# Three edits to an MLP pipeline: rounding on ScalarE, moments by the aggregation instruction, and incoming items spread over the light slots

## The reference, cut to what matters

```python
h = layernorm(x1)                       # x1 = x + mamba(...); plain, no weights
for blk in range(3):
    y = h @ W[2*blk].T + bias           # W: 4-bit weights times scales, plus a low-rank product
    y = gelu(layernorm(y) * gamma + beta)
    y = y @ W[2*blk+1].T + bias
    h = y + h
out = x1 + h
```

## Time and profile before

| | |
|---|---|
| device time, 3 runs | 1979.9 us median (1978.9 to 1980.2) |
| span of the profiled execution | 1980.0 us, the page's own figure |
| share of the span busy: PE, DVE, ACT, POOL | 92%, 78%, 64%, 60% |
| MLP items in the span | from about 1527 us on |
| TensorE clock granted there | below 1.0 until 1570 us, 1.0 after that |

### The profile page before, as it was taken

The page is one execution under the profiler, slowest core; times in us unless marked ns, Lnnn a source line. Parts: engine busy times, 40 slices in busy tenths (PEclk is TensorE's granted clock), DMA queues, the critical chain, the costliest instruction groups (busy, mean ns, idle before and its releaser), DMA issues. The chain is left out here.

```text
span 1980.0 us, 36525 instructions
## 1 busy us (share of the span) xinstructions
PE 1819.1 (92%) x12544; PEld 1380.2 (70%) x12544; DVE 1534.9 (78%) x3311; ACT 1260.0 (64%) x2221; POOL 1189.5 (60%) x1032
## 2 busy tenths in 40 slices
PE   5899999999999999999999999999974798988898
PEld 4577776777777777677777776777753677777776
DVE  4777888878778877777777777777635799999986
ACT  3677767776777666777677767777720455555554
POOL 2566666667666655555555555555540687868785
PEclk8899999999999989999999999999985899999999
DMA  4011111111111101111111111110005202012001
GB/s 141 22 39 38 39 48 58 37 42 37 37 37 37 48 28 49 59 39 44 37 37 37 37 48 58 37 42 26 28 11 148 86 1 95 34 41 89 33 12 43
DMA packets 87271, 91.96 MB, mean 46 GB/s; under 512 B 4928, under 2 KB 82448, under 8 KB 87184
## 3 DMA queue, kind: packets, MB, share of 16 engines
q1 hardware_dynamic: 79360, 79.46, 12.4%
q10 hardware_dynamic: 7824, 11.37, 2.3%
HBM read 57.26 MB, written 25.17 MB: 42 GB/s over the span
## 5 line engine op out<-in xcount | busy, mean ns | idle before, releaser
L860 POOL TENSOR_TENSOR L_xc<-L_xpad,L_vec 128x512 f32<-128x512 f32 x160 | 166.2, 1039 | 420.6 <-ACT L_xpad L659 401.3
L381 PE MATMUL L_front<-L_uhi,L_whi 128*128 128x512 f32 x576 | 247.2, 429 | 10.7 <-DVE L_xc L1078 7.3
L530 PE MATMUL L_mix<-L_wo,L_yg 128*128 128x256 f32 x1024 | 238.8, 387 | 3.2 <-POOL L_yg L852 3.2
L381 PE MATMUL L_front<-L_uhi,L_wlo 128*128 128x512 f32 x576 | 229.7, 399 | 0.0
L381 PE MATMUL L_front<-L_ulo,L_whi 128*128 128x512 f32 x576 | 229.7, 399 | 0.0
L1090 DVE TENSOR_TENSOR L_m<-L_dbank,L_gm 128x512 f32<-128x512 f32 x256 | 175.4, 685 | 69.6 <-ACT L_dbank L699 69.1
L530 PEld LDWEIGHTS L_mix<-L_wo,L_yg 128*128 128x128 f32 x1024 | 192.1, 193 | 35.0 <-issue 7.2
L852 POOL TENSOR_TENSOR L_yg<-L_yg,L_sz 128x512 f32<-128x512 f32 x128 | 164.3, 1284 | 85.9 <-DVE L_yg L1105 85.9
L659 ACT ACTIVATE L_xpad<-L_front,L_pbias 128x512 f32<-128x512 f32 x160 | 108.8, 681 | 131.8 <-PE L_front L381 130.9
L697 ACT ACTIVATE L_dbank<-L_dbank 128x512 f32<-128x512 f32 x256 | 148.8, 581 | 46.7 <-PE L_dbank L437 46.6
L1619 POOL TENSOR_TENSOR M_alo<-M_hT,M_ahi 128x512 fp32r<-128x512 f32 x96 | 125.6, 1312 | 75.1 <-DVE M_ahi L1681 75.1
(11 more groups left out here) (174 smaller groups left out, 4912.5 us busy)
## 6 DMA issues: line engine op xcount, KB each, us to landing
h<-L_hres SPq DMA_DIRECT2D x32, 512.0 KB, 3.0
L_hin<-in_x SPq DMA_DIRECT2D x16, 512.0 KB, 4.6
L_hres<-in_x SPq DMA_DIRECT2D x16, 512.0 KB, 3.8
L_cc<-L_xc ACTq DMA_DIRECT2D x64, 128.0 KB, 2.3
L_hin<-h SPq DMA_DIRECT2D x16, 512.0 KB, 4.7
L_hres<-h SPq DMA_DIRECT2D x16, 512.0 KB, 3.8
M_hin<-h SPq DMA_DIRECT2D x16, 512.0 KB, 6.4
M_xin<-in_x SPq DMA_DIRECT2D x16, 512.0 KB, 6.7
```

The costliest lines, as they stand in the source:

```text
L381: last = nc.tensor.matmul(to[:, :], ww[:, kd, tile * P:(tile + 1) * P], a[:, kd, :], start=i == 0, stop=i == len(passes) - 1)
L530: last = nc.tensor.matmul(mix[1 - s][:, (b % 2) * DM:(b % 2 + 1) * DM], yg[:, t, b * P:(b + 1) * P], wo[layer][:, t, :], start=t == 0, sto ...
L860: nc.gpsimd.tensor_tensor(xc[p][:, q, :].rearrange("p (b i) -> p b i", b=NB), xpad[:, q, :, 0:P], vector(layer, "conv_w", q * TAPS, 1).uns ...
```

## The change

1. round_h goes from DVE (tensor_copy) to ACT (activation Copy). In ACT's step n it stands for slot n, behind the copy_in of the same half. It now also waits for the second product of slot n-4 as a whole.
2. combine (seven instructions) is replaced by four bn_aggr, which reduce the six numbers of a bn_stats to mean and variance, then one tensor_scalar that adds EPS; for a block, another tensor_scalar that negates the mean.
3. add_x, in_stats, in_moments, norm_in (DVE) and scale_in (POOL) of a new item no longer stand in the steps of four neighbouring slots. A helper, entering, gives each stage of four items four steps two apart. For rounds after the first: add_x in steps 3, 5, 7, 9; in_stats, in_moments and scale_in in steps 4, 6, 8, 10; norm_in in steps 5, 7, 9, 11. The loads move to slot n+11 and stand behind the store of the same step. PE's order is not changed.
4. In DVE's step, both add_h now stand together ahead of norm_in and add_x, and the in_stats stand between the block_stats.

```diff
+        def entering(n, first, later):
+            turns = UNITS * BLOCKS
+            if 0 <= n + first < UNITS:
+                return n + first
+            round_, at = divmod(n - later, turns)
+            t = UNITS * (round_ + 1) + at // 2
+            return t if n >= later and at % 2 == 0 and at < 2 * UNITS and t < ITEMS else None
...
 @block.sync, step(n):
-                if n >= UNITS:
-                    load_item(n + 8)
                 store(n - 4)
+                load_item(n + 11)
...
 @block.scalar:
+            def round_h(n, kd):
...
+                if block_of(n) == 0:
+                    act.wait_ge(in_copied, 2 * item_of(n) + kd + 1)
+                else:
+                    act.wait_ge(second_done, 2 * (n - UNITS) + 2)
+                    act.wait_ge(h_added, 2 * (n - UNITS) + kd + 1)
+                nc.scalar.activation(ahi[u][:, kd, :], hT[u][:, kd, :], ACT.Copy).then_inc(h_hi, 1)
...
                 copy_in(n, 0)
+                round_h(n, 0)
                 normalise(n - 2, 3)
                 copy_in(n, 1)
+                round_h(n, 1)
                 gelu(n - 2, 0)
...
 @block.gpsimd, block_scale and step(n):
-                nc.gpsimd.tensor_tensor(shift[u][:, :, 0], mom[u][:, 5, :], rstd[u][:, :, 0], ALU.mult).then_inc(b_shift, 1)
+                nc.gpsimd.tensor_tensor(shift[u][:, :, 0], mean[u][:, :], rstd[u][:, :, 0], ALU.mult).then_inc(b_shift, 1)
-                scale_in(n + 2)
+                scale_in(entering(n, 2, 4))
...
 @block.vector, block_moments (in_moments alike, without the mean):
-                combine(nc, dve, stats[u], mom[u], var[u][:, :, 0], b_stats, b_mom, b_var, n, sign=-1)
+                dve.wait_ge(b_stats, NB * n + NB)
+                for b in range(NB):
+                    nc.vector.bn_aggr(mv[u][:, b, :], stats[u][:, b, :]).then_inc(b_mom, 1)
+                dve.wait_ge(b_mom, NB * n + NB)
+                nc.vector.tensor_scalar(var[u][:, :, 0], mv[u][:, :, 1], EPS, None, ALU.add).then_inc(b_var, 1)
+                nc.vector.tensor_scalar(mean[u][:, :], mv[u][:, :, 0], -1.0, None, ALU.mult).then_inc(b_mean, 1)
...
 @block.vector, step(n):
                 block_moments(n - 1)
                 add_h(n - 3, 0)
-                norm_in(n + 1)
-                in_stats(n + 2, 0)
                 add_h(n - 3, 1)
-                add_x(n + 7)
-                in_stats(n + 2, 1)
+                norm_in(entering(n, 1, 5))
+                add_x(entering(n, 7, 3))
+                in_stats(entering(n, 2, 4), 0)
+                in_stats(entering(n, 2, 4), 1)
                 add_out(n - 3, 0)
                 add_out(n - 3, 1)
-                in_stats(n + 2, 2)
-                in_stats(n + 2, 3)
                 block_stats(n, 0)
-                in_moments(n + 2)
+                in_stats(entering(n, 2, 4), 2)
                 block_stats(n, 1)
-                round_h(n + 1, 0)
+                in_stats(entering(n, 2, 4), 3)
                 block_stats(n, 2)
+                in_moments(entering(n, 2, 4))
                 block_stats(n, 3)
-                round_h(n + 1, 1)
```

More of the change, by code:

```diff
@@ L1412, in mlp_items @@
         stats0, var0, rstd0 = (sb(n, [P, NB, c]) for n, c in (("stats0_", 6), ("var0_", 1), ("rstd0_", 1)))
-        mom, mom0 = sb("mom", [P, 6, NB]), sb("mom0_", [P, 6, NB])
+        mv, mv0, mean = sb("mv", [P, NB, 2]), sb("mv0_", [P, NB, 2]), sb("mean", [P, NB])
         lin = [[ctx.enter_context(nc.psum_tensor(f"M_lin{u}{i}", [P, 512], F32)) for i in range(2)] for u in range(UNITS)]
@@ L1421, in mlp_items @@
         b_stats, b_mom, b_var, b_rstd, b_shift = (sem(n) for n in ("b_stats", "b_mom", "b_var", "b_rstd", "b_shift"))
-        b_normed = sem("b_normed")
+        b_mean, b_normed = sem("b_mean"), sem("b_normed")
         b_turned, b_gelu, g_hi, g_lo = (sem(n) for n in ("b_turned", "b_gelu", "g_hi", "g_lo"))
@@ L1436, in held, with held_by @@
             return hin[u][n // (UNITS * BLOCKS) % 2]
+        def held_by(t):
+            return hin[t % UNITS][t // UNITS % 2]
         def runs(n, m=None):
             return 0 <= n < SLOTS and m in (None, block_of(n))
+        def entering(n, first, later):
[5 more added lines that the diff above has]
+            return t if n >= later and at % 2 == 0 and at < 2 * UNITS and t < ITEMS else None
         block = ctx.enter_context(nc.Block())
@@ L1445, in load_item @@
             def load_item(n):
-                if not runs(n, 0):
+                if n < UNITS or not runs(n, 0):
                     return
@@ L1554, in copy_in @@
                 nc.scalar.activation(hT[u][:, kd, :], lin[u][kd][:, :], ACT.Copy).then_inc(in_copied, 1)
+            def round_h(n, kd):
+                if not runs(n):
+                    return
+                u = n % UNITS
+                if block_of(n) == 0:
[4 more added lines that the diff above has]
+                nc.scalar.activation(ahi[u][:, kd, :], hT[u][:, kd, :], ACT.Copy).then_inc(h_hi, 1)
             def normalise(n, b):
@@ L1596, in _, with scale_in @@
         def _(pool):
-            def scale_in(n):
-                if not runs(n, 0):
+            def scale_in(t):
+                if t is None:
                     return
-                t, u = item_of(n), n % UNITS
+                u = t % UNITS
                 pool.wait_ge(n0_var, t + 1)
@@ L1610, in block_scale @@
                 pool.wait_ge(b_rstd, n + 1)
-                pool.wait_ge(b_mom, 6 * n + 6)
-                nc.gpsimd.tensor_tensor(shift[u][:, :, 0], mom[u][:, 5, :], rstd[u][:, :, 0], ALU.mult).then_inc(b_shift, 1)
+                pool.wait_ge(b_mean, n + 1)
+                nc.gpsimd.tensor_tensor(shift[u][:, :, 0], mean[u][:, :], rstd[u][:, :, 0], ALU.mult).then_inc(b_shift, 1)
             def rest_h(n, kd):
@@ L1640, in _, with add_x @@
         def _(dve):
-            def add_x(n):
-                if not runs(n, 0):
+            def add_x(t):
+                if t is None:
                     return
[L1644 to L1649, removed]
+                u = t % UNITS
+                dve.wait_ge(h_in[u], 32 * (t // UNITS + 1))
+                nc.vector.tensor_tensor(held_by(t)[:, :, :], held_by(t)[:, :, :], xin[u][:, :, :], ALU.add).then_inc(x1_done, 1)
@@ L1650, in in_stats @@
+            def in_stats(t, b):
+                if t is None:
                     return
-                t, u = item_of(n), n % UNITS
+                u = t % UNITS
                 if b == 0:
                     dve.wait_ge(x1_done, t + 1)
-                nc.vector.bn_stats(stats0[u][:, b, :], held(n, u)[:, b, :]).then_inc(n0_stats, 1)
-            def in_moments(n):
-                if not runs(n, 0):
+                nc.vector.bn_stats(stats0[u][:, b, :], held_by(t)[:, b, :]).then_inc(n0_stats, 1)
@@ L1658, in in_moments @@
+            def in_moments(t):
+                if t is None:
                     return
[L1659 to L1663, removed]
+                u = t % UNITS
+                dve.wait_ge(n0_stats, NB * t + NB)
+                for b in range(NB):
+                    nc.vector.bn_aggr(mv0[u][:, b, :], stats0[u][:, b, :]).then_inc(n0_mom, 1)
+                dve.wait_ge(n0_mom, NB * t + NB)
+                nc.vector.tensor_scalar(var0[u][:, :, 0], mv0[u][:, :, 1], EPS, None, ALU.add).then_inc(n0_var, 1)
@@ L1664, in norm_in @@
+            def norm_in(t):
+                if t is None:
                     return
-                t, u = item_of(n), n % UNITS
+                u = t % UNITS
                 dve.wait_ge(n0_rstd, t + 1)
-                dve.wait_ge(n0_mom, 6 * t + 6)
+                dve.wait_ge(n0_mom, NB * t + NB)
                 for b in range(NB):
-                    last = nc.vector.tensor_scalar(normed[u][:, b, :], held(n, u)[:, b, :], mom0[u][:, 5, b:b + 1], rstd0[u][:, b, :],
+                    last = nc.vector.tensor_scalar(normed[u][:, b, :], held_by(t)[:, b, :], mv0[u][:, b, 0:1], rstd0[u][:, b, :],
@@ L1670, in norm_in @@
                                                    ALU.subtract, ALU.mult)
                 last.then_inc(n0_done, 1)
[L1673 to L1681, removed]
```

## The result

The changed kernel takes 1966.8 us (median of 4 runs, 1965.0 to 1968.3) against 1980.05 of the kernel before: a ratio of 0.9932, 95% interval 0.9918 to 0.9946. That is 13 us faster, where 27 were forecast.

The account below looks back on a forecast made before the run. DVE was taken to set the heavy slots, with PE's floor at 7.02 us a slot. Three rounds saving 5.5+2.55 each (24.2) plus 2.6 in the last light set gave 26.8 off 1980.0: 1953 us, range 1938 to 1970.

Parts of the forecast that it names:

- (a): Rival: near PE's floor, scale_in and add_x find gaps, light slots 7.2 us, heavy 9.3; 1940 us; chance 0.12.
- (b): Rival: heavy slots gain, light ones stay at 8.02 us; 1962 us; chance 0.22 shared with another rival.
- (c): Rival: norm_in held behind POOL's subtractions, odd light slots 12.2 us; 2007 us; chance 0.08, of which 0.06 a loss.
- part 4: Light slots with incoming work: add_x and norm_in in odd ones, scale_in in even; 7.7 us each, 2.55 saved a round.
- the rule weighed there: Small float32 DVE operations may share ports with POOL; by it norm_in would wait up to four times behind subtractions.
- DVE sets them: Heavy slots before the change: DVE busy 10.3 to 10.6 us against PE's 9.1, so DVE bounds them.
- Part 1: round_h to ACT: DVE loses 1.8 us a slot; the light slot's own loop falls from 7.58 to 7.15 us.
- Part 2: Moments by four bn_aggr: 0.35 us for four, 0.6 in all with the tensor_scalar, upper end 1.9.
- Part 3: Heavy slots: 9.4 us each, set by the new item's way within one PE step; 5.5 us saved a round.
- Part 4's other term: Even light slots: scale_in's second power in POOL's list adds 1.03 us, 15.3 for two slots.
- Loads: Issued behind the stores one by one, with two slots, some 15 us or more, until add_x; priced at nothing.

Follow-up runs that it names:

- a1: The changed kernel with only one of norm_in's four instructions, the rest of that normalisation left out; 1941.0 us.
- a2: The changed kernel with norm_in back in its old steps (11, 0, 1, 2) and between the two add_h; 1944.75 us.
- a3: The changed kernel with norm_in in its new steps but between the two add_h instead of behind both; 1947.1 us.
- b1: The kernel before with only round_h moved from DVE to ACT; 1971.1 us, ratio 0.9955.
- d1: c1 with POOL's scale_in back in its old steps (10, 11, 0, 1); 1946.7 us.
- b2: The kernel before with only the moments changed to bn_aggr; 1967.2 us, ratio 0.9939.
- d5: d4 with ACT doing the fourth normalise ahead of the first copy_in in slots with a new item; 1934.8 us.
- d4: d1 with norm_in behind both add_h, still in the old steps; 1938.9 us.
- c1: a2 with add_x, too, moved between the two add_h; 1943.8 us.
- d7: c1 with scale_in one step later (5, 7, 9, 11); 1940.3 us.
- b4: The kernel before with only the spread steps and DVE's new order, casts and seven-instruction moments staying on DVE; 1995.9 us, ratio 1.0085.
- a4: The changed kernel with norm_in moved from DVE to ACT as two pairs of Identity activations; 1954.2 us.
- b3: The changed kernel with round_h's two casts back on DVE where they stood; 1970.1 us.

## Why the prediction was wrong

It forecast 1953 and a gain of 27 us; 13 came. The direction held, the size did not. That 1966.8 lies in the range of 1938 to 1970 is partly luck: the range was drawn around (a) and (b), and what came is the mechanism of (c), for which the forecast had 2007.

**The step that failed** is in part 4: "Odd ones get add_x and (from 5) norm_in", with DVE's sum for an odd slot "0.6+1.45+1.4+1.2+1.5 = 6.15". The term 1.4 for norm_in was mis-sized: it is 5.31 where POOL is at its subtractions. The slot behind it takes 9.6 in place of 7.7, with DVE busy 9.51. In each of three rounds that is three light slots times 1.9, plus 0.9 in the first heavy slot (10.30 against 9.4), some 20 us. The other slots came out 1.9 a round below the forecast, 6 us, and the last round a little: 1953 + 20 - 6 = 1967. a1, a2 and a3 show it from three sides. The prediction had this mechanism as rival (c), with "four full ones are 5.2 us", and gave it 0.08. It discounted it because L1669 had never been long, while it had noted that mostly the power had run beside it. A row that shows an operation only beside one neighbour bounds nothing beside another.

Rival (c)'s total was wrong in turn. It added 5.2 us of waits to norm_in's own 1.4, where the four take 5.31 with their waits. It added 0.9 at add_x, which behind norm_in found POOL idle and ran in 1.21. And it took DVE's sum, 12.2, as the length of the slot, though norm_in begins in the slot before: the pair takes 16.9, not 12.2 + 7.7.

On the rule weighed there: the "GPSIMD Engine Reference" of the Trainium skill, section "Key points", says that POOL contends for SBUF interfaces with DVE instructions in a two-port mode or with two SBUF inputs. The prediction took the 403 ns for 256 elements as a sign that norm_in isn't in such a mode. Whether it is, no run here shows; that it is held, the 1364 ns do, so its duration alone didn't tell.

**What "DVE sets them" left out.** The prediction says this of the heavy slots. Its row of 10.49 has DVE busy only 8.44, and with the casts gone the slots keep their length (b1: 10.95, with DVE busy 7.75). A second way is as long as DVE's list: the new item's copy, rounding and rest_h, scale_in's power, and norm_in in front of the second add_h. The change shortens the heavy slots only because these last two leave them as well; d1, which puts both back there, takes 10.6.

**Part 1** held by amount and, in light slots, by its loop: the last round's slots take 7.01 (forecast 7.15, 7.58 before). Part 2 has a share in that, as alone it brings them to 7.18 (b2); part 1 alone brings them to 7.01 (b1). Over the whole part 1 alone is worth 8.5 us.

**Part 2** was right on bn_aggr: four in 0.38 us (0.35 forecast), 149 ns each in the median. The small tensor_scalar behind them are held at times, up to 0.91 and 1.32 us for a block and 1.10 for a new item. Alone part 2 is worth 12.4 us (b2).

**Part 3** was right for three of the four heavy slots: 9.2 (9.4 forecast). From turn_in to the first product it is 4.99 us (5.0 forecast):

```profile
1751.38 1.04 PE L1491 MATMUL M_lin<-M_ident,M_xin 128*128 128x128 f32 x8
...
1756.37 0.28 PE L1502 MATMUL M_lin<-M_bias,M_rowsel 96*128 96x256 bf16 x1
```

d5 shows that this term sets them: one activation out of it makes it 4.62 (4.99 in d4) and the slot 8.85 (9.21 in d4), nine times 0.36 and in the three first ones 0.2, which is the 4 us.

**Part 4's other term**, 1.03 for scale_in per two slots, holds only where scale_in shares a POOL step with a power that add_x stretches: a pair of light slots takes 14.96 in c1, 14.02 in d1 without scale_in there, and 14.16 in d7 with scale_in one step later. The forecast had the two in slots of different kinds. That its pair of 15.3 is close to a2's 15.12 is luck: there both costs fall into one slot. Moving norm_in (a2) is worth 20 to 22 us; that includes some of the clock dips described below.

**Loads** cost nothing, as forecast: no wait of DVE for a DMA stands in the rounds.

## What to carry to other kernels

Price a DVE instruction by what GpSimd does at that moment, not by its own row. Beside GpSimd's subtractions of 1.29 us, four small float32 tensor_scalar cost four of them here (5.31 us for 1.38); beside its power on four numbers they took 410 ns each (a3). Order such instructions so that they fall beside the short operations, and look whether what stands behind them is waited for, and whether a long one (add_x) stretches the short one in turn. Spreading work over lighter slots needs room there: in b4 DVE was busy 9.36 of 9.43 us in them and it cost 16 us, part of that busy time being waits for GpSimd (the runs don't say how large a part of the loss). So look at the neighbour's list as well as at its busy share.

## What the runs showed of the hardware

- bn_aggr on six numbers takes 149 ns in the median, four in 0.38 us, and never waited (maximum 184 ns) beside POOL's subtractions.
- The exclusion holds in both directions: add_x (1.21 us) stretched a power of 4 numbers from 1.01 to 1.81 us (c1), and a small multiplication from 0.20 to 0.75 (d1) and 1.27 (a4).
- TensorE's granted clock dipped three times in the first three rounds of the changed kernel, each time around the end of an idle wait of PE of about 2.3 us, while four other waits of that length left it at full speed. The windows around one of them:

```profile
1800.00:1803.00 3.00, 0.74 (x7) 0.53 (x5) 3.00 (x11) 2.37 (x6) 2.92 (x5) 1.00 0.00 0
1803.00:1806.00 3.00, 2.91 (x10) 2.33 (x11) 2.90 (x12) 0.60 (x2) 3.00 (x4) 0.61 0.00 0
1806.00:1808.00 2.00, 2.00 (x10) 1.83 (x9) 0.33 (x1) 1.54 (x3) 1.70 (x4) 0.72 0.00 0
```

The granted clock of 0.61 and 0.72 is a mean over full speed and half speed, 2.4 and 1.2 GHz. The slot of such a dip takes 10.4 to 10.9 us in place of 9.6. b1 dipped after each of its three waits of 2.8 us, b3 after three of its nine of 2.6, b4 after two of its three of 1.9. In the kernel before and in b2, whose waits from 1576 us on are at most 1.5 us, and in a1 to a4, c1 and d1 to d7, at most 1.2, there is no dip between 1576 us and the last 6 us of the span. That the idle waits cause the dips is an inference from this; no run was made to test it.
